# Left-over token tiles start two expert tiles later in a decoder layer's expert stage; first expert rows turned inside the last attention turn

## The chip, the cores and the metric

The kernel runs on one core of one Trainium2 chip. The metric is the device time of one execution in microseconds (us). Engines are named as in the profile: PE (TensorE, matmuls), DVE (VectorE), ACT (ScalarE), POOL (GpSimd) and SP, which only issues DMA transfers.

## What is computed

One post-norm decoder layer on x of shape 4 x 1024 x 256, in float32, with a context of 4 x 77 x 256:

```python
x = layernorm(x + self_attention(x, w_q, w_k, w_v, w_o))           # 16 heads of 16
x = layernorm(x + cross_attention(x, ctx, Wq, bq, Wk, bk, Wv, bv)) # one head of 256
# experts: 8, two for each token
gate = softmax(xf @ gate_w + gate_b); topv, topi = top_k(gate, 2); topv /= topv.sum(-1)
y = sum over e of combine[:, e] * (relu(xf @ w1[e] + b1[e]) @ w2[e] + b2[e])
x = layernorm(x + y)
```

## The kernel before

**Attention stage.** For each of 64 (batch, head) pairs there are 8 score tiles of 128 x 1024. Each tile is computed twice: `score_max` (L942) writes it to one of the two-bank PSUM tensors `pa[0]`, `pa[1]`, from where DVE takes the maxima (`maxima`, L1308), and `score_exp` (L954) writes its two halves to the banks `pb[0]`, `pb[1]`, from where ACT takes the exponentials (L1122). `sums` (L965) multiplies the exponentials with the values into `po`. Two score tiles are a "pair" (256 in all), eight pairs are a "turn" (32 in all). Maxima run `LEAD` = 8 pairs ahead, so the last turn has no `score_max` left. In every pair there is a place for one side job on PE in the bank `px` (`side`, L908): the projections of the next batch, and one step of the chain that a finished token tile `j` of 128 tokens goes through: `proj`, `turn_1`, `score` (cross scores, with a bias row added by a matmul of one row, L878), `turn_p`, `cross`, `turn_2`, `gate`. A side job waits until the reader of the one before has emptied `px` (`read_by`, L397). Token tile `j` is served `DELAY` = 9 turns after turn `j`, so 9 of the 32 token tiles are left over when attention ends: tile 23 (`MAIN_PROJ`) has its first steps to come, tile 22 (`MAIN_GATE`) its last ones.

**Expert stage.** 71 expert tiles of 128 rows follow. PE's order for expert tile t is `up(t+1)` (32 matmuls in three chunks), `turn_x(t+2)` (two transposes), `down(t)` (16 matmuls in three chunks). Between the chunks stand the steps of the left-over token tiles, `j = NT - TB + tile`, that is token tile 24 in expert tile 0. DVE copies the first-layer weights of the next expert into `w1_e` (`copy_w1`, L1650), two copies for a tile, the first of them not before `up` of the tile before has ended. The region of `w1_e` is that of the attention output of the batches 0 and 2. Which rows and which expert belong to a tile stands in a table: `early_tiles` (L1470) makes the entries of the first `EARLY` = 24 tiles from the batches 0 and 1, in turn 30; `late_tiles` (L1511) makes the other 47 after the last token tile is routed.

**Where attention ends.** The output of the last head goes out to memory and comes back turned (`store_out`, `load_out`), its row sums are inverted on DVE (`reciprocals`), written out (`spread_recs`), read back spread over the heads (`load_reps`, 512 KB), and POOL multiplies (`scale_heads`). Only then can token tile 24 be projected. On DVE the second pair of weight copies, `copy_w1(1, ..)`, stands behind `reciprocals`, and the loop over the expert tiles begins with a wait for `scaled`. Of the eight second-layer weights (1 MB each) two are loaded from SP and three from ACT at this place. ACT issues its three ahead of `copy_x(0)`, which PE needs for `up(0)`.

**Routing of the last batch.** In expert tile 9 DVE runs `counts`, `positions`, `rows`, `weights`, `pads` and all of `late_tiles`, ahead of the next `copy_w1`. `rows` writes `pos_i`, which the second scatters of the batch before still read, and waits for them:

```python
if b:
    dve.wait_ge(second_rows[b - 1], 16 * TB)
dve.tensor_copy(pos_i[:, :, :], pos_f[:, :, :]).then_inc(route, 1)
```

Of the kernel before, what the change touches and what calls it, by code (L numbers as in the profile page):

```python
# [116 lines left out]
def stream(nc, g):  # L117
# [44 lines left out]
    EARLY = 3 * TB  # L162
# [40 lines left out]
    with ExitStack() as st:  # L203
# [37 lines left out]
        fold_b = sb("fold_b", [1, B * C])  # L241
# [42 lines left out]
        pos_i = sb("pos_i", [P, 2, TB], I32)  # L284
        weight = sb("weight", [P, 2, TB])
        pad_i = sb("pad_i", [P, NE], I32)
        full_i = sb("full_i", [P, NE], I32)
        full, tiles, cum, early, step = (sb(n, [P, NE]) for n in ("full", "tiles_e", "cum", "early", "step"))
# [22 lines left out]
        pX = po[:, 0:D].rearrange("p (k t) -> p k t", k=KD)  # L311
# [85 lines left out]
        def read_by(p):  # L397
# [4 lines left out]
            if weights_step(p) is not None:  # L402
                return weights_made, weights_step(p) + 1
            if s == 0 and b:
                return rest_done, nth(b, p // TURN % TB)
# [12 lines left out]
        with nc.Block() as block:  # L418
            @block.sync
            def _(sp):  # L420
# [132 lines left out]
                for i in range(NH):  # L553
# [53 lines left out]
                for b in range(2):  # L607
                    sp.wait_ge(second_rows[b], 16 * TB)
                sp.wait_ge(table_1, len(TABLE))
                for tile in range(XS):  # L610
                    load_xg(tile)
                sp.wait_ge(v_ready, NH)
                settle(sp, g.settled_dma)
                load_w2(sp, 5)
                sp.wait_ge(b_done, 2 * TB * (NH - 2))
                settle(sp, g.settled_dma)
                load_w2(sp, 0)
                store_out(NH - 1)
                load_out(NH - 1)
                store_x2(MAIN_GATE)  # L620
                spread_recs(NH // PER - 1)
                load_reps(NH // PER - 1)
                load_x1(MAIN_PROJ + 1)
                for tile in range(FFN_TILES):
                    j = NT - TB + tile
# [7 lines left out]
                    if j + 1 < NT:  # L633
                        load_x1(j + 1)
                    if j - 1 < NT:
                        store_x2(j - 1)
                    if tile == TB + 2:
# [12 lines left out]
            def _(pool):  # L650
# [68 lines left out]
                def scatter_first(b, t):  # L719
# [3 lines left out]
                    pool.indirect_dma_start(g.xe_dram, bass.IndirectOffsetOnAxis(pos_i[:, 0, t:t + 1], 0),  # L723
                                            pay[b % 2][:, t, :], None, bounds_check=X_ROWS - 1).then_inc(first_rows[b], 16)

                def reweight(b):
                    pool.wait_ge(first_rows[b], 16 * TB)
                    pool.tensor_copy(pay[b % 2][:, :, D + 1], weight[:, 1, :]).then_inc(reweighted, 1)
# [3 lines left out]
                def scatter_second(b, t):  # L732
                    pool.indirect_dma_start(g.xe_dram, bass.IndirectOffsetOnAxis(pos_i[:, 1, t:t + 1], 0),  # L733
# [55 lines left out]
                scale_heads(NH // PER - 1)  # L789
                for tile in range(FFN_TILES):  # L790
                    j = NT - TB + tile
                    if tile:
                        scatter(tile - 1)
                    if j - 1 < NT:
                        spread_2(j - 1)
                    if j < NT:
                        spread_1(j)
                    if 2 <= tile < 6:
                        scatter_first(B - 2, 2 * (tile - 2))
                        scatter_first(B - 2, 2 * (tile - 2) + 1)  # L800
                    if 6 <= tile < 10:
                        if tile == 6:
                            reweight(B - 2)
                        scatter_second(B - 2, 2 * (tile - 6))
                        scatter_second(B - 2, 2 * (tile - 6) + 1)
                    if 10 <= tile < 14:
                        scatter_first(B - 1, 2 * (tile - 10))
                        scatter_first(B - 1, 2 * (tile - 10) + 1)
                    if 14 <= tile < 18:
                        if tile == 14:  # L810
                            reweight(B - 1)
                        scatter_second(B - 1, 2 * (tile - 14))
                        scatter_second(B - 1, 2 * (tile - 14) + 1)
# [9 lines left out]
            def _(pe):  # L823
# [48 lines left out]
                def score(j):  # L872
# [5 lines left out]
                    pe.matmul(out, g.ones[0:1, :], fold_b[:, cols], start=False, stop=True).then_inc(scored, 1)  # L878
# [28 lines left out]

                def side(p):  # L908
# [8 lines left out]
                    if weights_step(p) is not None:  # L917
                        cross_weights(weights_step(p))
                    elif s == 0:
# [34 lines left out]
                def score_exp(n):  # L954
# [57 lines left out]
                def turn_x(tile):  # L1012
                    pe.wait_ge(xg_in[tile % XS], 16 * (tile // XS + 1))
                    if tile:
                        pe.wait_ge(x_taken, tile)
                    for k in range(KD):
                        mm = pe.transpose(pX[:, k, :], xg[tile % XS][:, k * P:(k + 1) * P], g.ident[:, :])  # L1017
                    mm.then_inc(turned_x, 1)

# [37 lines left out]
                turn_x(1)  # L1057
                score(MAIN_PROJ)
                gate(MAIN_GATE)
                up(0, CHUNKS[2])  # L1060
                for tile in range(FFN_TILES):
                    j = NT - TB + tile
# [4 lines left out]
                    if j - 1 < NT:  # L1067
# [3 lines left out]
                    if j - 1 < NT:  # L1071
# [3 lines left out]
                    if j < NT:  # L1075
                        pe.wait_ge(mixed, j)
                        proj(j)
                    if tile == 1:
                        ranks(B - 2)
                    if tile == TB + 1:  # L1080
# [6 lines left out]
                    if j - 1 < NT:  # L1087
                        if j < NT:
                            pe.wait_ge(added, j + 1)
                        if tile == 1:  # L1090
# [3 lines left out]
                    if j < NT:  # L1094
# [3 lines left out]
                    if j < NT:  # L1098
                        score(j)
                    if j - 1 < NT:  # L1100
# [3 lines left out]
            def _(act):  # L1104
# [12 lines left out]
                def exponentials(n):  # L1117
                    for half in range(2):
# [3 lines left out]
                        act.activation(ex[:, n % 4, half * HALF:(half + 1) * HALF], pb[half][:, :], ACT.Exp,  # L1122
# [47 lines left out]

                def behind(p):
# [5 lines left out]
                    if n is not None:  # L1177
                        if n < KD:
                            act.wait_ge(weights_mm, n + 1)
                            act.activation(c_k[:, n, :], px[:, 0:B * C], ACT.Identity, bias=c_bk[:, n:n + 1]  # L1180
                                           ).then_inc(weights_made, 1)
                    elif s == 0 and b:
# [38 lines left out]
                def copy_x(tile):  # L1221
                    act.wait_ge(turned_x, tile + 1)
                    if tile >= 2:
                        act.wait_ge(up_done, tile - 1)
                    act.copy(xgT[tile % 2][:, :, :], pX).then_inc(x_taken, 1)

# [25 lines left out]
                for tile in range(FFN_TILES):  # L1252
                    j = NT - TB + tile
# [548 lines left out]
```

## Time and profile before

| | |
|---|---|
| median of 3 runs | 1553.7 us (1552.85 to 1553.7) |
| the profiled execution | 1560.21 us, of which 1558.4 us are the span of its instructions |
| PE busy | 1470.9 us, 94% of the span |
| DVE, ACT, POOL busy | 967.4, 821.0, 388.7 us |
| chain that ended last | PE 86%, DVE 5%, DMA 3%, issue 2%, SP's queue 2%, ACT 1% |
| attention stage | to about 941 us |
| expert stage | to about 1515 us, then the last layer norm |

The span is cut into 40 slices of 39 us in the page; a digit is the busy share of a slice in tenths. A timeline row reads: start, duration, engine, line, operation, output<-inputs, count, and in brackets how long the engine had been idle and what ended that. A row of the chain reads: start, duration, what. "PEclk" is the granted clock of PE as a share of 2.4 GHz, so 0.5 is 1.2 GHz.

### The profile page before, as it was taken

The numbers are of one execution on the slowest core, as the hardware profiler recorded it, in microseconds if no ns is written. First come the engines' busy times: TensorE is split into PE (matmuls) and PEld (weight loads), VectorE is DVE, ScalarE is ACT, GpSimd is POOL, SyncE is SP. The second block draws the span as 40 slices with busy tenths as digits, with TensorE's granted clock in tenths as the row PEclk, the third lists the DMA queues.
The fourth block names the chain that finished last, engine by engine and source line by source line (L and its number), as shares of the span: only waits on it lengthen the run. The fifth ranks groups of instructions, "written<-read, shape, count | busy, mean of one in ns | idle before, by whom it ended". The sixth has DMA issues, their size and how long they took to land.

```text
span 1558.4 us, 32241 instructions
## 1 busy us (share of the span) xinstructions
PE 1470.9 (94%) x10682; PEld 928.9 (60%) x10682; DVE 967.4 (62%) x1678; ACT 821.0 (53%) x1966; POOL 388.7 (25%) x677
## 2 busy tenths in 40 slices
PE   7899999999999999999999996998999999999990
PEld 3244443444444444444444445887999999999990
DVE  6677777778888888788888862555332333333326
ACT  3466677776676766676766772332333333333330
POOL 1211121212212214411115211354522122122123
PEclk9799999999999999999999998999999999999995
DMA  5224122324433323322343216223322222222216
GB/s 157 82 64 140 57 83 86 115 88 127 123 103 112 104 78 103 97 79 61 83 124 103 76 36 184 57 66 90 75 50 36 42 35 39 39 36 40 37 22 222
DMA packets 112195, 130.57 MB, mean 84 GB/s; under 512 B 26048, under 2 KB 89808, under 8 KB 111904
## 3 DMA queue, kind: packets, MB, share of 16 engines
q1 hardware_dynamic: 93760, 101.68, 21.9%
q0 software_dynamic: 14000, 19.48, 7.0%
q10 hardware_dynamic: 4272, 7.34, 1.3%
q8 instruction: 89, 1.46, 0.4%
q14 instruction: 74, 0.61, 0.1%
HBM read 76.51 MB, written 51.94 MB: 82 GB/s over the span
## 4 chain that ended last, share of the span: by engine, by line
PE 86%; DVE 5%; DMA 3%; issue 2%; SPq 2%; ACT 1%; POOL 0%; DVEq 0%; POOLq 0%; another core or an unknown queue 0%; ACTq 0%
PE pa L1028 16%; PE pb L961 15%; PE po L975 15%; PE pb L1039 15%; PE pa L949 13%; PE px L826 3%; PE px L862 2%; DVE neg L1313 2%; PE px L832 1%; SPq L435 1%; PE po L1017 1%; ACT w_sb L1122 1%; PE px L899 1%; PE px L877 1%; PE px L878 1%
## 5 line engine op out<-in xcount | busy, mean ns | idle before, releaser
L1313 DVE TENSOR_REDUCE neg<-pa 128x1 f32<-128x1024 f32 x512 | 614.6, 1217 | 141.8 <-PE pa L949 130.8
L1122 ACT ACTIVATE w_sb<-pb 128x512 f32<-128x512 f32 x1024 | 555.9, 595 | 207.0 <-PE pb L961 201.2
L1233 ACT ACTIVATE space<-pa,b1T_sb 128x128 f32<-128x128 f32 x568 | 154.7, 383 | 325.4 <-PE pa L1028 324.6
L961 PE MATMUL pb<-w_sb 99*128 99x512 bf16 x1024 | 314.4, 384 | 9.1 <-ACT w_sb L1122 4.9
L949 PE MATMUL pa<-w_sb 96*128 96x512 bf16 x1024 | 301.6, 385 | 8.1 <-DVE neg L1313 7.3
L1028 PE MATMUL pa<-xgT,attn_t 128*128 128x128 f32 x2272 | 274.3, 279 | 12.7 <-issue 4.9
L1028 PEld LDWEIGHTS pa<-xgT,attn_t 128*128 128x128 f32 x2272 | 271.4, 195 | 17.0 <-issue 8.5
L975 PE MATMUL po<-w_sb,space 128*32 128x256 f32 x4096 | 274.1, 385 | 0.5 <-ACT w_sb L1122 0.5
L1039 PE MATMUL pb<-w_sb,space 128*128 x1136 | 260.1, 380 | 0.0
L1039 PEld LDWEIGHTS pb<-w_sb,space 128*128 128x128 f32 x1136 | 209.5, 191 | 25.0
L1654 DVE COPY attn_t<-w_sb 128x1024 f32 x142 | 99.0, 697 | 171.9 <-PE pa L1028 156.1
L783 POOL DMA_INDIRECT x<-space,y_tag x71 | 110.4, 1554 | 376.7 <-DVE space L1671 307.8
L961 PEld LDWEIGHTS pb<-w_sb 99*128 99x128 bf16 x1024 | 82.2, 97 | 202.2 <-ACT w_sb L1122 140.8
L975 PEld LDWEIGHTS po<-w_sb,space 128*32 128x32 f32 x4096 | 106.8, 109 | 137.5 <-issue 90.2
L949 PEld LDWEIGHTS pa<-w_sb 96*128 96x128 bf16 x1024 | 96.3, 100 | 120.4 <-DVE neg L1313 27.1
L1667 DVE TENSOR_TENSOR space<-pb,b_sb 128x256 f32<-128x256 f32 x71 | 30.2, 425 | 139.2 <-PE pb L1039 132.9
L679 POOL TENSOR_TENSOR neg_parts<-neg,ones 128x8 bf16<-128x8 f32 x64 | 13.1, 205 | 262.8 <-DVE neg L1313 262.8
L714 POOL TENSOR_TENSOR dev_B<-mv_B,eps 128x1 f32<-128x1 f32 x32 | 8.6, 268 | 256.0 <-DVE mv_B L1377 256.0
L826 PE MATMUL px<-w_sb,space 128*128 128x512 f32 x96 | 46.9, 611 | 0.0
L862 PE MATMUL px<-woT_sb,attn_t 128*128 128x256 f32 x128 | 34.2, 390 | 6.0 <-DVE pay L1366 6.0
L723 POOL DMA_INDIRECT x_by_expert<-pay,pos_i x32 | 34.0, 1063 | 14.6 <-issue 10.2
L733 POOL DMA_INDIRECT x_by_expert<-pay,pos_i x32 | 33.9, 1061 | 11.2 <-issue 7.5
(194 smaller groups left out, 986.3 us busy)
## 6 DMA issues: line engine op xcount, KB each, us to landing
xg<-x_by_expert SPq DMA_DIRECT2D x71, 130.0 KB
attention_out<-space SPq DMA_DIRECT2D x64, 128.0 KB
w_sb<-w SPq DMA_DIRECT2D x16, 512.0 KB, 5.0
q_parts<-w_sb SPq DMA_DIRECT2D x48, 128.0 KB
w_sb<-q_parts SPq DMA_DIRECT2D x64, 96.0 KB, 2.5
w_sb<-k_parts SPq DMA_DIRECT2D x64, 96.0 KB, 2.5
k_parts<-w_sb SPq DMA_DIRECT2D x45, 128.0 KB
w_sb<-w SPq DMA_DIRECT2D x5, 1024.0 KB, 8.4
```

The lines of the kernel that those rows point to most:

```text
L783: pool.indirect_dma_start(g.x2_dram, bass.IndirectOffsetOnAxis(y_tag[tile % TAGS][:, 0:1], 0), y[tile % 2], None, bounds_check=Y_ROWS - 1, ...
L826: mm = pe.matmul(out[:, :], w_qk[:, which, k, m * P:(m + 1) * P], x[:, k, cols], start=k == 0, stop=k == KD - 1)
L862: mm = pe.matmul(px[:, 0:D], g.attn_t[:, b % 2, k, t * P:(t + 1) * P], g.woT_sb[:, k, :], start=k == 0, stop=k == KD - 1)
L949: mm = pe.matmul(pa[n % 2][:, half * HALF:(half + 1) * HALF], qs[i % RING][0:STACK, t * P:(t + 1) * P], ks[i % RING][0:STACK, half * HALF: ...
L961: pe.matmul(pb[half][:, :], ks[i % RING][:, t * P:(t + 1) * P], qs[i % RING][:, half * HALF:(half + 1) * HALF], start=True, stop=True).the ...
L975: mm = pe.matmul(po[32 * j:32 * j + VW, 0:QC], vs[i % 2][:, t, :], ex[:, n % 4, j * QC:(j + 1) * QC], start=t == 0, stop=t == TB - 1, tile ...
L1028: mm = pe.matmul(pH[tile % 2][:, f, :], w1_e[:, k, f * P:(f + 1) * P], xgT[tile % 2][:, k, :], start=k == 0, stop=k == KD - 1)
L1039: mm = pe.matmul(pY[tile % 2], hT[tile % 2][:, f, :], g.w2_sb[:, bass.ds(e, 1), f, :].rearrange("p e d -> p (e d)"), start=f == 0, stop=f ...
L1122: act.activation(ex[:, n % 4, half * HALF:(half + 1) * HALF], pb[half][:, :], ACT.Exp, scale=SCALE).then_inc(e_done, 1)
L1233: ins = act.activation(hT[tile % 2][:, f, :], pH[tile % 2][:, f, :], ACT.Relu, bias=g.b1_sb[:, bass.ds(e * FT + f, 1)])
L1313: dve.tensor_reduce(neg[i % 2][:, t:t + 1], pa[n % 2][:, :], AX.X, ALU.max, negate=True).then_inc(max_done, 1)
L1654: dve.tensor_copy(w1_e[:, k], g.w1_sb[:, bass.ds(e, 1), k].rearrange("p e f -> p (e f)")).then_inc(w1_copied, 1)
```

## The change

1. **Two tiles later.** `SHIFT = 2`: the steps of the left-over token tiles stand in expert tile `j + 2 - 24`. Tiles 22 and 23 are finished inside the loop (in expert tiles 1 and 2) and no longer ahead of it; routing of batch 2 moves from expert tile 1 to 3, that of batch 3 from 9 to 11, its scatters from tiles 10 to 17 to tiles 12 to 19. DVE's wait for `scaled` moves behind the weight copies of expert tile 1, with `result(0)` behind it; `scale_heads` of the last heads moves to POOL's tile 1.
2. **First rows turned early.** `turn_x(0)` and `turn_x(1)` become side jobs of the pairs 0 and 3 of the last turn, in `px`, and `copy_x(0)`, `copy_x(1)` follow the exponentials there. The first three `load_xg` stand in SP's iteration 60, `early_tiles` in turn 29. `EARLY` is 25. SP's two loads of second-layer weights stand at the end of its iteration 63.
3. **The start of the stage.** After the last `sums`, PE does `proj(23)`, waits for the maxima and does the whole of `up(0)`. DVE's first copies wait for `proj(23)` alone.
4. **Second sets of buffers.** `pos_i` and `weight` are doubled, so that `rows` and `weights` wait for the scatters of two batches before.
5. **`late_tiles` and `pads` spread.** Counts to weights of batch 3 are in expert tile 11; `pads` and stage 0 of `late_tiles` in 12, stage 1 in 13, stage 2 in 14.
6. **Bias over 128 rows.** `fold_b` is 128 rows high, zero but for its first row, and the matmul that adds it takes 128 rows.
7. **Last scores in the banks of the maxima.** From the second pair of the last turn on, `score_exp` uses the four banks of `pa` in place of the two of `pb`.

```diff
-    EARLY = 3 * TB
+    EARLY = 3 * TB + 1
+    SHIFT = 2
+    def feeds(p):
+        turn, s = divmod(p, TURN)
+        return (0, 3).index(s) if turn == TURNS - 1 and s in (0, 3) else None
+    def in_pa(n):
+        return n >= 2 * (PAIRS - LEAD) + 2
...
+        pX = [bank[:, 0:D].rearrange("p (k t) -> p k t", k=KD) for bank in (px, px, po)]
+        def score_bank(n, half):
+            return pa[n % 2][:, half * HALF:(half + 1) * HALF] if in_pa(n) else pb[half][:, :]
...
+                    if i == NH - 4:
+                        for b in range(2):
+                            sp.wait_ge(second_rows[b], 16 * TB)
+                        sp.wait_ge(table_1, len(TABLE))
+                        for tile in range(XS):
+                            load_xg(tile)
+                    if i == NH - 1:
+                        sp.wait_ge(v_ready, NH)
+                        settle(sp, g.settled_dma)
+                        load_w2(sp, 5)
+                        sp.wait_ge(b_done, 2 * TB * (NH - 2))
+                        settle(sp, g.settled_dma)
+                        load_w2(sp, 0)
...
-                    pe.matmul(out, g.ones[0:1, :], fold_b[:, cols], start=False, stop=True).then_inc(scored, 1)
+                    pe.matmul(out, g.ones[:, :], fold_b[:, cols], start=False, stop=True).then_inc(scored, 1)
...
-                        if n:
+                        if in_pa(n):
+                            pe.wait_ge(max_done, NH * TB - 1 + n % 2)
+                            pe.wait_ge(e_done, 2 * n - 3 + half)
+                        elif n:
                             pe.wait_ge(e_done, 2 * n - 1 + half)
-                        pe.matmul(pb[half][:, :], ks[i % RING][:, t * P:(t + 1) * P],
+                        pe.matmul(score_bank(n, half), ks[i % RING][:, t * P:(t + 1) * P],
...
-                pe.wait_ge(max_done, NH * TB)
-                pe.wait_ge(e_done, 2 * NH * TB)
                 pe.wait_ge(mixed, MAIN_PROJ)
                 proj(MAIN_PROJ)
-                pe.wait_ge(o_out, NH)
-                turn_x(0)
-                pe.wait_ge(added, MAIN_PROJ + 1)
-                turn_2(MAIN_GATE)
-                up(0, CHUNKS[0])
-                pe.wait_ge(c_copied, MAIN_GATE + 1)
-                turn_1(MAIN_PROJ)
-                up(0, CHUNKS[1])
-                turn_x(1)
-                score(MAIN_PROJ)
-                gate(MAIN_GATE)
-                up(0, CHUNKS[2])
+                pe.wait_ge(max_done, NH * TB)
+                for chunk in CHUNKS:
+                    up(0, chunk)
+                pe.wait_ge(e_done, 2 * NH * TB)
                 for tile in range(FFN_TILES):
-                    j = NT - TB + tile
+                    j = NT - TB + tile - SHIFT
...
                 for e in (1, 2, 3):
                     load_w2(act, e)
-                copy_x(0)
-                copy_2(MAIN_GATE)
-                copy_1(MAIN_PROJ)
-                copy_x(1)
-                soft(MAIN_PROJ)
...
-                    if b:
-                        dve.wait_ge(second_rows[b - 1], 16 * TB)
-                    dve.tensor_copy(pos_i[:, :, :], pos_f[:, :, :]).then_inc(route, 1)
+                    if b >= 2:
+                        dve.wait_ge(second_rows[b - 2], 16 * TB)
+                    dve.tensor_copy(pos_i[b % 2][:, :, :], pos_f[:, :, :]).then_inc(route, 1)
...
+                g.w1_in.wait(dve, 0, g.w1_loads)
+                e = number(dve, 0, 1)
+                dve.wait_ge(projected, MAIN_PROJ + 1)
+                for k in range(KD):
+                    copy_w1(0, k, e)
                 norm_2(MAIN_GATE)
                 add(MAIN_PROJ)
                 measure_1(MAIN_PROJ)
-                g.w1_in.wait(dve, 0, g.w1_loads)
-                for k in range(KD):
-                    copy_w1(0, k)
-                norm_1(MAIN_PROJ)
-                reciprocals(NH // PER - 1)
                 keep(0)
                 keep(1)
-                dve.wait_ge(scored, MAIN_PROJ + 1)
-                logits(MAIN_GATE)
-                cross_max(MAIN_PROJ)
-                best(MAIN_GATE)
+                norm_1(MAIN_PROJ)
+                e = number(dve, 1, 1)
+                reciprocals(NH // PER - 1)
                 for k in range(KD):
-                    copy_w1(1, k)
-                dve.wait_ge(scaled, NH // PER)
+                    copy_w1(1, k, e)
...
+                    if tile == 1:
+                        dve.wait_ge(scaled, NH // PER)
+                        result(0)
...
                         pads()
-                        late_tiles()
-                    if tile == TB:
-                        hot_experts(B - 1)
+                    if tile >= TB + SHIFT + 2:
+                        late_tiles(tile - TB - SHIFT - 2)
```

## Rows read from the trace of the kernel before

**Rows 1.** The page, part 2: PE's busy tenths in 40 slices

```profile
PE   7899999999999999999999996998999999999990
```

**Rows 2.** Chain that ended last, 320 to 917 us, shares by line

```profile
by line: PE pb L961 25.7%; PE po L975 25.2%; PE pa L949 22.8%; DVE neg L1313 4.3%; PE px L826 4.0%; PE px L862 3.0%; issue 2.7%; PE px L832 2.0%; PE px L899 1.2%; ACT w_sb L1122 1.2%; PE px L886 1.1%; PE px L877 1.1%; PE px L878 1.0%; PE px
```

**Rows 3.** Stretches: length, PE, PEld, DVE, ACT, POOL busy, PEclk, DMA share, GB/s

```profile
916.70:941.00 24.30, 21.49 (x197) 9.37 (x196) 6.07 (x20) 18.62 (x39) 2.94 (x10) 1.00 0.22 64
941.00:970.20 29.20, 16.91 (x96) 15.25 (x97) 7.28 (x23) 6.80 (x24) 4.44 (x7) 0.84 0.69 209
...
1091.60:1500.00 408.40, 408.40 (x2815) 384.96 (x2814) 127.47 (x282) 139.16 (x513) 101.27 (x71) 1.00 0.24 42
```

**Rows 4.** Chain that ended last, end of attention: start, us, what

```profile
937.01 0.39 PE pb L961
...
939.90 1.11 PE po L975 x16
...
941.43 6.67 DMA attention_out<-space
...
948.56 5.70 DMA o_sums<-attention_out
...
954.28 0.56 DVE o_sums L1324
...
964.68 2.35 POOL attn_t L700
...
967.87 2.08 PE px L862 x4
```

**Rows 5.** Timeline of PE, 941 to 1000 us

```profile
947.68 2.93 PE L1028 MATMUL pa<-xgT,attn_t 128*128 128x128 f32 x12 [4.70 <-ACT xgT L1225]
...
957.89 2.90 PE L1028 MATMUL pa<-xgT,attn_t 128*128 128x128 f32 x12 [3.10 <-DVE attn_t L1654]
...
993.53 1.13 PE L862 MATMUL px<-woT_sb,attn_t 128*128 128x256 f32 x4 [1.78 <-DVE pay L1366]
```

**Rows 6.** Timeline of SP's queue, 930 to 945 us

```profile
938.04 1.02 SPq L379 DMA_DIRECT2D w_sb<-w  x2
```

**Rows 7.** Timeline of ACT, 940 to 948 us

```profile
941.14 6.08 ACTq L379 DMA_DIRECT2D w_sb<-w  x3
```

**Rows 8.** Chain that ended last, three kinds of expert tiles

```profile
1033.78 1.44 PE pa L1028 x12
...
1044.71 1.44 PE pa L1028 x12
...
1080.22 4.91 issue
1085.13 6.42 PE pa L1028 x32
...
1095.23 3.57 PE pa L1028 x32
...
1102.47 3.57 PE pa L1028 x32
```

**Rows 9.** Timeline of DVE, 1075 to 1085 us

```profile
1075.49 0.17 DVE L1447 CAST pos_i<-pos_f 128x16 int32<-128x16 f32 x1 [2.53 <-DMA x_by_expert<-pay,pos_i]
...
1081.57 0.18 DVE L1548 TENSOR_SCALAR table<-x 128x47 int32<-128x47 f32 x1
...
1083.58 1.46 DVE L1654 COPY attn_t<-w_sb 128x1024 f32 x2 [0.42 <-issue]
```

**Rows 10.** Timeline of PE in single matmuls, around one score bias

```profile
1054.34 0.39 PE L877 MATMUL px<-fold,turned_B 128*128 128x77 f32 x2
...
1054.45 0.28 PE L877 MATMUL px<-fold,turned_B 128*128 128x77 f32 x1
...
1054.66 0.44 PE L878 MATMUL px<-fold_b,ones 1*128 1x77 f32 x2
...
1055.03 0.28 PE L899 MATMUL px<-gate_w_sb,turned_C 128*128 128x8 f32 x1
```

More of the change, by code:

```diff
@@ L283, in stream @@
         pos_f = sb("pos_f", [P, 2, TB])
-        pos_i = sb("pos_i", [P, 2, TB], I32)
-        weight = sb("weight", [P, 2, TB])
+        pos_i = [sb(f"pos_i{i}", [P, 2, TB], I32) for i in range(2)]
+        weight = [sb(f"weight{i}", [P, 2, TB]) for i in range(2)]
         pad_i = sb("pad_i", [P, NE], I32)
         full_i = sb("full_i", [P, NE], I32)
-        full, tiles, cum, early, step = (sb(n, [P, NE]) for n in ("full", "tiles_e", "cum", "early", "step"))
+        tiles, cum, early, step = (sb(n, [P, NE]) for n in ("tiles_e", "cum", "early", "step"))
+        full = cum
         b2_sb = sb("b2_sb", [P, NE, D])
@@ L403, in read_by @@
                 return weights_made, weights_step(p) + 1
+            if feeds(p) is not None:
+                return x_taken, feeds(p) + 1
             if s == 0 and b:
@@ L1219, in _ @@
                 take_output(NH - 1)
[L1221 to L1225, printed above, removed]
                 def relu(tile):
@@ L1529, in late_tiles @@
-                    dve.tensor_scalar(step[:, NE - 1:NE], early[:, NE - 1:NE], -1.0, None, ALU.mult).then_inc(table_2, 1)
-                    dve.wait_ge(table_2, tabled_2("step_last"))
-                    dve.tensor_tensor(tiles[:, :], tiles[:, :], step[:, :], ALU.subtract).then_inc(table_2, 1)
-                    dve.tensor_tensor(past, wide(slots, False, n), wide(cum[:, :], True, n), ALU.is_ge).then_inc(table_2, 1)
-                    dve.wait_ge(table_2, tabled_2("past"))
-                    dve.tensor_reduce(expert, past, AX.X, ALU.add).then_inc(table_2, 1)
@@ L1535, in late_tiles @@
-                    dve.wait_ge(table_2, tabled_2("expert"))
-                    dve.tensor_tensor(past, past, wide(tiles[:, :], True, n), ALU.mult).then_inc(table_2, 1)
-                    dve.wait_ge(table_2, tabled_2("weighted"))
-                    dve.tensor_reduce(before_e, past, AX.X, ALU.add).then_inc(table_2, 1)
-                    dve.wait_ge(table_2, tabled_2("before"))
-                    dve.tensor_tensor(before_e, slots, before_e, ALU.subtract).then_inc(table_2, 1)
-                    dve.wait_ge(table_2, tabled_2("row"))
@@ L1542, in late_tiles @@
-                    dve.tensor_scalar(before_e, before_e, early[:, 0:1], None, ALU.add).then_inc(table_2, 1)
-                    dve.wait_ge(table_2, tabled_2("row_0"))
-                    dve.tensor_scalar(before_e, before_e, float(P), None, ALU.mult).then_inc(table_2, 1)
-                    dve.wait_ge(table_2, tabled_2("rows_128"))
-                    dve.scalar_tensor_tensor(g.table[:, 0, EARLY:], expert, float(ROWS_E), before_e, ALU.mult,
-                                             ALU.add).then_inc(table_2, 1)
@@ new lines, in late_tiles @@
+                    if stage == 1:
+                        dve.tensor_tensor(past, wide(slots, False, n), wide(cum[:, :], True, n), ALU.is_ge).then_inc(table_2, 1)
+                        dve.wait_ge(table_2, tabled_2("past"))
+                        dve.tensor_reduce(expert, past, AX.X, ALU.add).then_inc(table_2, 1)
+                        dve.wait_ge(table_2, tabled_2("expert"))
+                        dve.tensor_tensor(past, past, wide(tiles[:, :], True, n), ALU.mult).then_inc(table_2, 1)
+                        dve.wait_ge(table_2, tabled_2("weighted"))
+                        dve.tensor_reduce(before_e, past, AX.X, ALU.add).then_inc(table_2, 1)
@@ new lines, in late_tiles @@
+                    if stage == 2:
+                        dve.wait_ge(table_2, tabled_2("before"))
+                        dve.tensor_tensor(before_e, slots, before_e, ALU.subtract).then_inc(table_2, 1)
+                        dve.wait_ge(table_2, tabled_2("row"))
+                        dve.tensor_scalar(before_e, before_e, early[:, 0:1], None, ALU.add).then_inc(table_2, 1)
+                        dve.wait_ge(table_2, tabled_2("row_0"))
+                        dve.tensor_scalar(before_e, before_e, float(P), None, ALU.mult).then_inc(table_2, 1)
+                        dve.wait_ge(table_2, tabled_2("rows_128"))
+                        dve.scalar_tensor_tensor(g.table[:, 0, EARLY:], expert, float(ROWS_E), before_e, ALU.mult,
+                                                 ALU.add).then_inc(table_2, 1)
+                        dve.tensor_scalar(g.table[:, 1, EARLY:], expert, float(NE - 1), None, ALU.min).then_inc(table_2, 1)
@@ L1605, in side_taken @@
                         measure_2(j)
-                    if turn == TURNS - 2 and s in (1, 4, 5, 6):
+                    if turn == TURNS - 3 and s in (1, 4, 5, 6):
                         early_tiles((1, 4, 5, 6).index(s))
```

202 lines of the change are left out of this document (105 added, 97 removed).

## Prediction

> **What bounds the kernel now.** I read the page first: PE is busy for nine tenths or more in nearly every slice, with dents in the first slices, about 940 to 1090 us, and at the end [rows 1]. So time comes either out of PE's own work or out of those dents. The chain that ended last tells which work counts in the attention stage: from 320 to 917 us over three quarters of it are the three large matmul groups of PE, and the side jobs stand on it too (L877 1.1%, L878 1.0%) [rows 2]. A saving on PE there is mostly a saving of time. The table of stretches sizes the dents [rows 3]. In the last attention turn (916.7 to 941.0) neither PE (21.5 of 24.3 us) nor ACT (18.6) is full: they wait for each other. From 941.0 to 970.2 PE is busy for 16.9 of 29.2 us, part of it at 1.2 GHz (mean granted clock 0.84). From 1091.6 to 1500 PE is full, so there only less PE work would help. In the chain of the tiles there is a second hole, 4.91 us at 1080.22, and behind it 32 matmuls that took 6.42 us [rows 8].
>
> A profiled execution takes 1560.2 us, the runs shown 1553.7: I sum against the former and take off the 6.5 us at the end. Less than 0.2% (3 us) is about what a measurement of this kernel can't tell from no change.
>
> **Part 7, the last turn.** With two banks, the second half of a tile's scores waits for the exponential of the tile before. So the chain of a pair holds this matmul (0.39 us at 937.01) between ACT's last exponential and the sums [rows 4]. With `pa` it is ready before. A matmul of 512 columns takes about 0.2 us of this 0.39 net, since the rest is the latency that the sums then have themselves. `in_pa` starts at the second pair, and the pair with `proj` and `gate` is full on PE, so six pairs gain 0.2 us: **1.3 us**. Bounds: nothing, if ACT's added copies eat it, and 7 x 0.39 = 2.7. ACT is idle for 24.3 - 18.6 = 5.7 us in these eight pairs [rows 3], so two copies of some 0.4 us fit in. The two turnings add 0.4 us to a PE that waits there for 2.8.
>
> **Parts 1 to 3, the start of the expert stage.** Call the end of the last sums E (939.90 + 1.11 = 941.0). Before, `down(0)` begins after `proj(24)` and a turning, at 967.87 + 2.08 + 0.4 = 970.4 [rows 4], so at E + 29.4. Three waits fill this. ACT issues three loads for 6.08 us [rows 7] before it copies the first rows, and `up(0)` starts at 947.68, at half clock. `up(1)` waits for weight copies until 957.89 [rows 5]. `proj(24)` waits for the last output, its reciprocals, their way out and back and POOL's 2.35 us [rows 4].
>
> After: `proj(23)` about 1.0 us (the four matmuls of 1.13 at 993.53 [rows 5]), DVE's two copies 1.46 [rows 9] with some 0.3 of latency, `up(0)` 3.57 at full clock [rows 8]: it ends at E + 6.3. Is it at full clock? PE waits 1.8 us ahead of it. The wait of 1.78 at 993.53 left the next four matmuls at 1.13 us, while after the longer standstill ahead of 967.87 four such took 2.08 [rows 4, 5]. So I count it as warm; if not, it costs 1.5.
>
> `up(1)` needs the next copies, and these stand behind `reciprocals` as before. The chain to it is the store of 6.67 us and the way back of 5.70: inversion at E + 13.3 [rows 4]. These two ran among 5 MB of weights. SP's two, issued at 938.04 [rows 6] on the queue that the store uses too, now go some 4 us earlier, since the table reads and row loads in front of them are gone. ACT's three still go out beside the store. I take a store of about 4 and a way back of 5.2, so inversion at E + 9.7. Bounds: E + 13.3 (nothing gained) and E + 6.3 (any earlier, and the copies wait for the end of `up(0)` anyway). Add 0.56, 1.46 and 0.2: `up(1)` starts at E + 11.9. PE has then idled 5 us, so its first 12 matmuls take 2.9 us instead of 1.44 [rows 5, 8], 5.1 for all; with a turning, `down(0)` starts at E + 17.2 instead of E + 29.4. This is 12.2 us earlier, but the token steps that were done in the hole now stand in the loop: one set of them, the difference between a tile with steps (1044.71 - 1033.78 = 10.93) and one without (1102.47 - 1095.23 = 7.24), 3.7 [rows 8]. Gain **8.5 us**, from 4.9 (late inversion) to 12.1.
>
> What goes on behind it: the way out and back of the reciprocals and POOL's product took 964.68 + 2.35 - 954.28 = 12.8 us [rows 4]. DVE now waits for it after the copies of tile 1, PE at `proj(24)` in tile 2. From the inversion to the first are 2.2 + 5.1 + 0.2 + 3.5 + 3.6 + 1.5 = 16 us. It is covered with 3 us to spare; each us beyond this costs one. On POOL `scatter(0)` stands behind it, which nothing needs for two tiles.
>
> **Parts 4 and 5, the hole at 1080.** DVE waits 2.53 us for the second scatters of batch 2, ends the table only at 1081.57 + 0.18, and makes the copies for the next tile at 1083.58 [rows 9], when PE has stood since 1080.22 [rows 8]. It costs 4.91 plus 6.42 - 3.57 = 2.85 at half clock: **7.8 us**. After, the wait is on batch 1, done long before. The work from 1075.66 to 1081.75, 6.1 us, goes into four tiles, the counts and positions with about 1 us of it into tile 11 (some 3.4 us in all), at most 2.4 in any other. A tile without steps has DVE busy for 31% of 7.24 us, 2.3 [rows 3], so both fit in 7.24 us. The copies may come up to 2 us after the `up` that frees their room before PE waits. Bound: 0, if the hole comes back.
>
> **Part 6, the bias.** From the start of the last fold matmul (1054.45) to the one behind the two bias matmuls (1055.03) are 0.58 us for three matmuls; the fold matmuls, with 128 rows and as many columns, follow each other by 0.11 [rows 10]. Three of those take 0.33, so a score gains 0.25. All nine scores in the expert loop are PE-bound: 2.2 us. Of those in attention the chain holds 1.0% of 597 us, 6.0 us, at 0.37 (1054.66 to 1055.03) apiece, that is 16: 4.0 us. Together **6.3 us** [rows 2, 10], between 0 (the extra time has to do with the product, not with its rows) and 32 x 0.25 = 8.
> The Trainium skill has rules for both ends. "TensorE: Matmul & The Clock Gate", section on LDWEIGHTS, says that loading weights depends on the columns and not on the rows; by it alone the term is nothing and the time 6.3 us later. "TensorEngine Tiling (Array Packing)", Key Properties, says that a change of tiling mode drains the engine; if one row counts as such a mode, this is the 0.25. The gaps of 0.21 and 0.20 on either side of the bias, against 0.11, agree with the second.
>
> **At nothing:** `early_tiles` in turn 29 (the same DVE work among the same maxima, one turn earlier); SP's waits in iteration 60 (ahead of `load_rows` of the next head; the table is made a turn, batch 1 scattered two turns before; uncovered they would stall attention); EARLY at 25; the memset at the start.
>
> **Sum.** 1.3 + 8.5 + 7.8 + 6.3 = 23.9. 1560.2 - 23.9 = 1536.3 profiled, less 6.5 gives **1530**.
>
> **Rivals.**
> (a) The forecast, 1530; with the bounds of the start 1526 to 1534. Chance 0.60.
> (b) The bias gains nothing: 1536. For it: the trace of before holds no bias of 128 rows, so the cause of the gaps is not shown. Against: the gaps [rows 10]. Chance 0.12.
> (c) The hole comes back in tiles 11 to 14, as DVE's copies slip behind the routing again: up to 1538. For it: one of the pieces still has 3.4 us, and the copies' room is free for only 3.7 us ahead of need. Chance 0.12.
> (d) `down(0)` waits for all eight weights. ACT's three start at E as before, and the old trace only says that they were in by E + 29. If they come that late, the gain of the start is lost: 1538.5. Chance 0.07.
> (e) Slower: the last scatters stand two tiles later, in tiles 16 to 19, and SP may load tile 25's rows only after them (in tile 22). Batch 2's were in at 1075.49 [rows 9], one tile after the last was issued, so two tiles are to spare. If POOL's queue makes them late, PE stands for as long. It turns the sign from 24 + 2 x 7.24 = 38 us of lateness on; with six tiles (43 us) PE stands 29 us: 1559. Chance 0.03.
> (f) More than forecast (early inversion, all scores on the path): 1523. Chance 0.06.
>
> The range of 0.8 leaves out the tips of (e), (f) and part of (c) and (d) together: 1521 to 1541. Faster by over 0.2%: all but (e) and a mishap of several, 0.95; same 0.02; slower 0.03.
>
> **What would show it.** In the profile after: the stretch of the last turn under 23.5 us; `up(0)` in one piece some 3 us after the last sums at full clock; a hole ahead of `up(1)` ended by DVE's copies; `down(0)` at E + 17; tiles with steps of 10.7 instead of 10.93; no idle PE between tile 10 and the end; bias matmuls 0.11 apart. It is wrong if a new idle time of PE ended by DVE or a load stands at tiles 11 to 25, if the inversion comes at E + 13 or later, or if bias matmuls keep their 0.58.

## The result and the profile after

The changed kernel takes 1537.8 us (median of 4 runs, 1537.5 to 1538.2) against 1553.7: ratio 0.9895, 95% interval 0.9878 to 0.9912. That is 16 us less, where 24 were forecast. The measured time lies outside the forecast's own band of 1526 to 1534 and inside the whole range of 1521 to 1541. The first line below is the busy line of the page of after, the second PE's slices; they answer to [rows 1]. The dent in the slice of 1052 to 1091 us is gone, that at the end of attention is smaller (7 tenths busy where it was 6).

```profile
PE 1458.3 (95%) x10682; PEld 921.3 (60%) x10682; DVE 968.6 (63%) x1679; ACT 820.5 (53%) x1966; POOL 388.0 (25%) x677
...
PE   7899999999999999999999997999999999999990
```

The stretches of after, cut at its own marks: last turn, hole at the start of the expert stage, `down(0)` to `down(11)`, the tiles behind. They answer to [rows 3], but the first row starts at the first `sums` of the last turn, 3.0 us later in the turn than the row of 24.30 us there. From this mark before took 20.21 + 1.11 = 21.3 us and after 19.9.

```profile
914.73:934.60 19.87, 17.92 (x178) 8.78 (x179) 3.51 (x15) 16.32 (x37) 2.00 (x8) 1.00 0.40 118
934.60:952.53 17.93, 10.20 (x71) 9.61 (x71) 4.87 (x13) 2.54 (x9) 1.31 (x4) 0.81 0.79 245
952.53:1068.69 116.16, 111.19 (x751) 100.23 (x750) 62.85 (x209) 40.47 (x148) 49.56 (x60) 0.99 0.28 64
1068.69:1490.00 421.31, 421.31 (x2907) 397.22 (x2906) 138.31 (x333) 142.04 (x528) 111.42 (x78) 1.00 0.27 45
```

The chain of after from the last sums to `down(0)`, which answers to [rows 4]:

```profile
933.46 1.11 PE po L1010 x16
934.60 0.38 ACT space L1146
935.00 3.77 DMA attention_out<-space
938.85 0.33 SPq L500
939.23 6.04 DMA o_sums<-attention_out
945.58 0.30 DVEq L397
945.88 0.23 DVE attn_t L1671
946.31 0.69 DVE attn_t L1671
947.13 5.34 PE pa L1055 x32
952.47 0.22 PE po L935 x2
952.69 3.46 PE pb L1066 x16
```

```profile
945.29 0.55 DVE L1338 RECIPROCAL o_sums<-o_sums 128x64 f32<-128x64 f32 x1 [5.43 <-DMA o_sums<-attention_out]
```

That last row, from DVE's timeline, is the inversion. With E = 934.6: the store takes 3.77 us instead of 6.67, the way back 6.04 instead of 5.70, the inversion comes at E + 10.7 and `down(0)` at E + 18.0. PE's timeline of the same place, and of expert tile 3, in which the routing of batch 2 delays `proj`, answers to [rows 5]:

```profile
937.19 3.81 PE L1055 MATMUL pa<-xgT,attn_t 128*128 128x128 f32 x32 [1.59 <-DVE attn_t L1671]
947.13 5.34 PE L1055 MATMUL pa<-xgT,attn_t 128*128 128x128 f32 x32 [6.14 <-DVE attn_t L1671]
...
993.92 1.34 PE L882 MATMUL px<-woT_sb,attn_t 128*128 128x256 f32 x4 [2.33 <-DVE pay L1380]
...
995.48 2.77 PE L1066 MATMUL pb<-w_sb,space 128*128 x6
```

`up(0)` runs in one piece at full clock. The wait of 2.33 us at 993.92 is followed by six matmuls of `down` in 2.77 us, at half clock. In the kernel before the table delayed `up(12)`, in the second expert tile behind the routing (tile 9). The same place of after is `up(14)` behind `down(12)`, and PE's timeline shows it with no gap and at full clock; it answers to the 4.91 and 6.42 us of [rows 8]:

```profile
1075.94 3.62 PE L1066 MATMUL pb<-w_sb,space 128*128 x16
1079.39 3.73 PE L1055 MATMUL pa<-xgT,attn_t 128*128 128x128 f32 x32
```

The score bias in single matmuls of after, which answers to [rows 10]: 0.34 us from the start of the last fold matmul to the start of the one behind the bias, where it was 0.58.

```profile
964.04 0.28 PE L897 MATMUL px<-fold,turned_B 128*128 128x77 f32 x1
...
964.15 0.39 PE L898 MATMUL px<-fold_b,ones 128*128 128x77 f32 x2
...
964.38 0.22 PE L919 MATMUL px<-gate_w_sb,turned_C 128*128 128x8 f32 x1
```

### The profile page after: what moved, and what is told of

The parts are those of the page before. It is cut to its first block, busy times and chain, and to the rows that moved or that the text cites. A ratio compares the mean times of both kernels' runs of the same rounds, so it can differ in the third digit from the quotient of the medians.

```text
span 1536.0 us, 32052 instructions
## 1 busy us (share of the span) xinstructions
PE 1458.3 (95%) x10682; PEld 921.3 (60%) x10682; DVE 968.6 (63%) x1679; ACT 820.5 (53%) x1966; POOL 388.0 (25%) x677
## 4 chain that ended last, share of the span: by engine, by line
PE 83%; DVE 6%; issue 3%; DMA 2%; ACT 2%; SPq 2%; DVEq 0%; POOL 0%; POOLq 0%; ACTq 0%
PE pa L1055 16%; PE pb L1066 15%; PE po L1010 14%; PE pb L996 14%; PE pa L981 13%; PE px L846 3%; DVE neg L1327 2%; PE px L882 2%; ACT w_sb L1139 2%; PE px L852 1%; SPq L451 1%; PE po L935 1%; PE px L919 1%; PE px L906 1%; DVE w_sb L1768 1%
## 5 line engine op out<-in xcount | busy, mean ns | idle before, releaser
L1139 ACT ACTIVATE w_sb<-pb 128x512 f32<-128x512 f32 x996 | 540.3, 594 | 198.8 <-PE pb L996 196.5
L996 PE MATMUL pb<-w_sb 99*128 99x512 bf16 x996 | 306.6, 383 | 5.5 <-DMA w_sb<-minus_maxima 2.7
L1055 PE MATMUL pa<-xgT,attn_t 128*128 128x128 f32 x2272 | 270.1, 276 | 7.7 <-DVE attn_t L1671 7.7
L1055 PEld LDWEIGHTS pa<-xgT,attn_t 128*128 128x128 f32 x2272 | 267.6, 193 | 11.8 <-issue 8.3
L1671 DVE COPY attn_t<-w_sb 128x1024 f32 x142 | 93.7, 697 | 132.1 <-PE pa L1055 130.6
L741 POOL DMA_INDIRECT x_by_expert<-pay,pos_i x32 | 33.5, 1046 | 15.1 <-issue 10.7
L751 POOL DMA_INDIRECT x_by_expert<-pay,pos_i x32 | 33.2, 1038 | 11.4 <-issue 7.8
```

The source lines that it names most:

```text
L996: pe.matmul(score_bank(n, half), ks[i % RING][:, t * P:(t + 1) * P], qs[i % RING][:, half * HALF:(half + 1) * HALF], start=True, stop=True ...
L1055: mm = pe.matmul(pH[tile % 2][:, f, :], w1_e[:, k, f * P:(f + 1) * P], xgT[tile % 2][:, k, :], start=k == 0, stop=k == KD - 1)
L1671: dve.tensor_copy(w1_e[:, k], g.w1_sb[:, bass.ds(e, 1), k].rearrange("p e f -> p (e f)")).then_inc(w1_copied, 1)
```

## The experiments

Four marks in each trace make the comparison sharper than the medians: the start of the first `sums`, of the last `sums`, of `down(0)` and of `down(11)`. The last `sums` are marked by their start, 1.1 us ahead of E, which is their end. What lies ahead of the first mark varies by itself: 56.5 to 60.1 us in fourteen profiled executions.

| us | e1 (before) | after | difference |
|---|---|---|---|
| up to the first sums | 57.75 | 59.88 | varies |
| to the last sums | 874.92 | 873.58 | -1.3 |
| to `down(0)` | 30.54 | 19.07 | -11.5 |
| to `down(11)` | 121.47 | 116.17 | -5.3 |
| to the end | 466.83 | 467.30 | +0.5 |
| from the first sums on | 1493.76 | 1476.12 | -17.6 |

**e1: the kernel before once more.**

> The kernel before, unchanged, profiled once more. In the profiled execution of before, six attention turns (18 to 20, 27, 28 and a part of 17) were 0.1 to 1.6 us longer than those of the kernel after, 4.8 us in all, and this execution lay 6.5 us above the median. Theory 1: these long turns belong to single executions; this profile then has turns 19 and 20 at 28.4 us, 27 and 28 at 26.4, and lies near 1554. Rival: they belong to the kernel before and something in the change took them away; then they are here again and the profile is near 1560.

1553.9 us against 1554.1 beside it, ratio 1.0001 (0.9992 to 1.0011); span 1551.5 us. Turns 19, 20, 27 and 28 last 28.38, 28.38, 26.39 and 26.39 us, the same as in after. Theory 1 holds: the 4.9 us were that one execution's. The profile that the prediction read was 6.5 us above the median for this and for 2.3 us at the start, and to take these 6.5 us off the sum was right.

**e2: the bias over 128 rows alone.**

```diff
-        fold_b = sb("fold_b", [1, B * C])
+        fold_b = sb("fold_b", [P, B * C])
...
-                    pe.matmul(out, g.ones[0:1, :], fold_b[:, cols], start=False, stop=True)
+                    pe.matmul(out, g.ones[:, :], fold_b[:, cols], start=False, stop=True)
```

> The kernel before with the bias over 128 rows alone. My prediction put 2.2 us on the nine scores of the expert stage and 4.0 us on those of the attention stage, 6.3 us in all. Theory now: in the attention stage the 0.25 us on PE are swallowed two matmuls later, where score_max waits for DVE's maxima, so turns 9 to 16 stay at 28.38 us and only the 2.2 us of the expert stage come: 1551.5. Rival (the prediction): turns of 28.1 us and 1547.5. Second rival (rows cost nothing): 1553.7.

1552.2 against 1554.1, ratio 0.9988 (0.9979 to 0.9997). In the expert stage a tile with steps takes 10.63 us instead of 10.93 and the stretch `down(0)` to `down(11)`, with eight scores, 118.73 instead of 121.47: 2.7 us. In attention the turns 10 to 16 stay at 28.37 us (28.38), and turn 26 grows from 28.11 to 28.48. So the numbers of e2's theory hold and the prediction's 4.0 us for the attention stage fall. But what swallows them is not the wait of `score_max` for the maxima. First the chain of e1 around one score of turn 24, then that of e2 around the same one:

```profile
740.17 0.40 PE px L877 x4
740.57 0.37 PE px L878 x2
740.94 0.54 PE pa L949 x2
741.48 0.43 PE pb L961 x2
741.91 1.00 PE po L975 x16
742.91 0.54 PE pb L961 x2
```

```profile
742.32 0.24 DVE cneg L1352
...
742.80 0.19 ACT pr L1158
743.00 0.99 ACT w_sb L1122 x2
743.98 0.04 issue
744.03 0.39 PE pb L961
744.42 0.43 PE pa L949 x2
```

In e1 everything stands on PE. In e2 the chain leaves PE: DVE's maxima, the cross maximum behind them (`cneg`), ACT's softmax that waits for it, and the two exponentials that wait behind this on ACT in program order. The timelines of e1 (first four rows) and e2 (last four) show why nothing is gained:

```profile
740.20 1.23 DVE L1313 TENSOR_REDUCE neg<-pa 128x1 f32<-128x1024 f32 x1
741.35 0.23 DVE L1352 TENSOR_REDUCE cneg<-px 128x1 f32<-128x77 f32 x1
741.92 1.08 ACT L1122 ACTIVATE w_sb<-pb 128x512 f32<-128x512 f32 x2
742.85 0.61 PE L961 MATMUL pb<-w_sb 99*128 99x512 bf16 x2
...
741.17 1.23 DVE L1313 TENSOR_REDUCE neg<-pa 128x1 f32<-128x1024 f32 x1
742.32 0.23 DVE L1352 TENSOR_REDUCE cneg<-px 128x1 f32<-128x77 f32 x1
742.90 2.18 ACT L1122 ACTIVATE w_sb<-pb 128x512 f32<-128x512 f32 x4
743.56 0.85 PE L961 MATMUL pb<-w_sb 99*128 99x512 bf16 x2
```

The score begins at 740.00 in e1 and at 740.98 in e2. In both, `cneg` starts 1.3 us behind that, since DVE is at maxima of 1.23 us that stand ahead of it, and not when PE is done with the score. So ACT's second exponential ends 3.0 us behind the score's beginning in both (and in every turn from 9 to 29 but 18 and 26). In e1 this is 743.00, and the second of the two L961 matmuls, which needs its bank, starts at about 743.08 (the end of the pair less 0.38 us for one), so this second path ended 0.08 us ahead of the one on PE. In e2 PE is there about 0.25 us earlier and waits 0.24 us, and the matmul starts at 744.03, as far behind the score's beginning as in e1 to within 0.03 us. The chain doesn't show what comes second. In turn 26 `cneg` starts 2.06 us behind the score's beginning in e1 and 2.43 in e2: that is the 0.37 us by which this turn grows.

**e3: the hole alone.** The second sets of `pos_i` and `weight`, and `pads` and `late_tiles` over tiles 10 to 12 of the kernel before:

```diff
-                        pads()
-                        late_tiles()
...
+                    if tile == TB + 2:
+                        pads()
+                    if tile >= TB + 2:
+                        late_tiles(tile - TB - 2)
```

> The kernel before with the second sets of pos_i and weight and with pads and late_tiles spread over tiles 10 to 12, nothing else. Theory: the hole at tile 10 of 4.91 us idle and 2.85 us at half clock goes, and nothing takes its place: 7.8 us less, 1546. Rival: part of it comes back as smaller waits in tiles 9 to 12, or the executions outside the profile have a smaller hole: 3 to 5 us less.

1547.1 against 1554.1, ratio 0.9953 (0.9939 to 0.9966). `down(0)` to `down(11)` takes 113.41 us instead of 121.47, 8.1 less, and each tile behind tile 9 takes 7.25. Tile 10 itself gives 7.65 of it (14.90 in e1); the other 0.4 lies in the tiles before, and `down(0)` came 0.5 later, so from the first sums on it is 7.6. The medians give 7.0. The theory holds.

**e4: the last scores in `pb`.**

```diff
-        return n >= 2 * (PAIRS - LEAD) + 2
+        return False and n >= 2 * (PAIRS - LEAD) + 2
```

> The kernel after with the last scores in the two banks of pb, as before. Theory: the last turn is 1.5 us longer (20.2 us between the first and last sums instead of 18.7), and all behind it shifts by as much: 1539.3. Rival: the start of the expert stage hangs on the output's way to memory and back, which doesn't care for 1.5 us of PE: then it still shifts, since the output is finished by the same sums; only if the way back is bound by the weight loads do less than 0.5 us remain.

Between the first and last sums of the last turn lie 20.21 us instead of 18.73, and from the first sums to the end 1478.07 instead of 1476.12. The theory holds in the trace. The median, 1537.2 (0.9893, 0.9878 to 0.9908), can't show it: the start varies by more.

**e5 and e6: which half of the hole.** e5 puts `pads` and all of the table into tile 11 and keeps the two sets; e6 has one set and keeps the table spread.

```diff
-                    if tile == TB + SHIFT + 2:
-                        pads()
-                    if tile >= TB + SHIFT + 2:
-                        late_tiles(tile - TB - SHIFT - 2)
+                    if tile == TB + SHIFT + 1:
+                        pads()
+                        for stage in range(3):
+                            late_tiles(stage)
```

> The kernel after with pads and all of late_tiles in expert tile 11 behind the routing of the last batch, in place of tiles 12 to 14; pos_i and weight stay doubled. Theory: the table is the larger cause of the hole. DVE then has about 3.4 + 6.1 us in one tile and some 5.8 us of room, so PE stands for 2 to 4 us ahead of up(12) and loses up to 2.9 more at half clock: 3 to 6 us more than the kernel after. Rival: without the wait of 2.53 us there is room enough and nothing changes.

```diff
-        pos_i = [sb(f"pos_i{i}", [P, 2, TB], I32) for i in range(2)]
+        pos_i = [sb(f"pos_i{i}", [P, 2, TB], I32) for i in range(1)] * 2
...
-                    if b >= 2:
-                        dve.wait_ge(second_rows[b - 2], 16 * TB)
+                    if b:
+                        dve.wait_ge(second_rows[b - 1], 16 * TB)
```

> The kernel after with one pos_i and one weight, so that DVE waits again for the second scatters of batch 2 in tile 11, with the table still spread. Theory: a wait of some 2.5 us alone fits into DVE's room, PE does not stand: same as after (0 to 0.5 us more). Rival: the wait alone makes part of the hole: 2 us or more.

PE in e5, at `up(14)`:

```profile
1080.57 5.44 PE L1055 MATMUL pa<-xgT,attn_t 128*128 128x128 f32 x32 [2.07 <-issue]
```

2.07 us idle and 5.44 - 3.73 = 1.7 at half clock: the trace from one `down` to the next has 11.18 us instead of 7.25, 3.9 more, as the theory has it, and the median is 1540.2 (0.9914, 0.9897 to 0.9930), 2.4 above after. DVE in e6:

```profile
1073.15 0.17 DVE L1461 CAST pos_i<-pos_f 128x16 int32<-128x16 f32 x1 [2.54 <-DMA x_by_expert<-pay,pos_i]
```

The same wait as in [rows 9], 2.54 us, and PE has no gap behind it: every tile from 11 on takes 7.24 to 7.25 us. The median is 1535.4 (0.9883, 0.9867 to 0.9900). So the table at once makes a hole of 3.9 us alone, the wait makes none alone, and only with the table does it lengthen it to 7.7 us. The second sets of buffers, in the kernel after, are worth nothing that shows.

**e7: weight copies ahead of the reciprocals.**

```diff
                 e = number(dve, 1, 1)
-                reciprocals(NH // PER - 1)
                 for k in range(KD):
                     copy_w1(1, k, e)
+                reciprocals(NH // PER - 1)
```

> The kernel after with the second pair of weight copies (copy_w1(1)) ahead of reciprocals on DVE, nothing else. Theory: the 6.14 us of PE's wait ahead of up(1) come from the order on DVE alone: up(1) starts at E + 8.2 instead of E + 12.6 (E is the end of the last sums) and at full clock, down(0) at E + 12.1 instead of E + 18. But the reciprocals' way and POOL's product still end at E + 24, and DVE waits for them in tile 1 ahead of cross_max(23), so part comes back as a wait of PE ahead of turn_p(23) in tile 2: 3 to 4 us less than after in all. Rival: down(0) waits for the second-layer weights, at E + 14 or later, and less than 2 us remain.

The timeline of PE in e7, with E = 934.4:

```profile
942.42 3.81 PE L1055 MATMUL pa<-xgT,attn_t 128*128 128x128 f32 x32 [1.59 <-DVE attn_t L1671]
946.07 0.38 PE L935 MATMUL po<-ident,xg 128*128 128x128 f32 x2
948.84 1.64 PE L1066 MATMUL pb<-w_sb,space 128*128 x3 [2.38 <-DMA w_sb<-w]
```

`up(1)` starts at E + 8.0 as the theory has it. But then PE waits for the last second-layer weights until E + 14.4, and `down(0)` takes 5.36 us, most of it at half clock, instead of 3.62. From the last sums to the end it is 600.7 us against 602.5 of after: the rival was right. 1535.7 us, 0.9887 (0.9870 to 0.9903).

**e8: e7, a later wait for `scaled`, and routing over two tiles.**

```diff
-                    if tile == 1:
-                        dve.wait_ge(scaled, NH // PER)
-                        result(0)
                     if MAIN_GATE <= j - 1 < NT:
...
+                    if tile == 1:
+                        dve.wait_ge(scaled, NH // PER)
+                        result(0)
...
+                    if tile == SHIFT + 2:
                         rows(B - 2)
                         weights(B - 2)
```

> The run e7 with two more moves on DVE: the wait for scaled and result(0) stand behind logits, cross_max and best in tile 1, and rows and weights of batch 2 stand in tile 4 instead of tile 3. Theory: the rest of the 6 us arrives too, and tile 3 loses its wait of 2.3 us ahead of proj with the half clock behind it (13.9 us down to 12 or less): 7 to 8.5 us less than after. Rival: rows and weights only make tile 4 as long as tile 3 was, and the way of the reciprocals decides at proj(24) in tile 2: 4 us less than after, like e7.

1540.1 us (0.9916, 0.9899 to 0.9932): 4.4 us more than e7 and 2.3 more than after, and neither theory had it. DVE in e8:

```profile
968.95 0.17 DVE L1677 COPY y_tag<-xg 128x2 int32<-128x2 int32 x1 [3.76 <-DMA x<-space,y_tag]
```

With `result(0)` later its scatter is later (issued at 964.96, E + 31.9, against 961.46, E + 27.1, in e7), and `keep(4)`, which uses the same `y_tag` again, waits 3.76 us for it, ahead of `mix(23)`; PE stands for 3.95 us ahead of `proj(24)`. The split routing gave nothing worth having: tiles 3, 4, 5 took 11.7, 12.0, 11.9 us instead of 13.9, 11.5, 10.6.

**e9: the first of the three waits of before.**

```diff
+                copy_x(0)
                 for e in (1, 2, 3):
                     load_w2(act, e)
-                copy_x(0)
```

> The kernel before with copy_x(0) ahead of ACT's three weight loads, nothing else. It takes away the first of the three waits at the end of attention: up(0) then starts some 5 us earlier (E + 1.5 to E + 2.5, by DVE's weight copies). Theory: this alone is worth nothing, since up(1) still waits for the copies behind reciprocals and proj(24) for the reciprocals' way out and back, both of which hang on the last output: within 0.5 us of before, with the three loads and the store shifted by less than 1. Rival: each wait of PE in this stretch has its own worth, and 3 to 5 us come.

`up(0)` starts at 941.00, E + 5.1 instead of E + 6.7, held by DVE's weight copies, and not by E + 2.5 as expected. `down(0)` is 30.4 us behind the last sums, as before (30.5). 1553.7 us, 0.9999 (0.9989 to 1.0008): nothing, as the theory says.

**e10 and e11: after and e7 side by side.**

> The kernel after, unchanged, to stand beside e11 on one chip. 1537.8 as before; from the last sums to the end 602.5 us in its profile, or 1 to 1.5 less where PE stays at full clock behind the wait of 2.3 us in expert tile 3 (as it did in e5 and e6).

> The run e7 once more: copy_w1(1) ahead of reciprocals. From e7: down(0) at E + 15.5, ended by the last second-layer weights, and 1.9 us less than after from the last sums to the end. Expected 1.5 to 2.5 us less than e10.

e10: 1536.7 us (0.9891, 0.9875 to 0.9908), 602.9 us from the last sums on. e11: 1534.5 us (0.9883, 0.9866 to 0.9899), 599.7. The difference is 2.2 us in the medians and 3.2 in the traces: e11 is the fastest version here, about 1.2% under before. The same place of e10 that cost after half clock:

```profile
993.99 1.13 PE L882 MATMUL px<-woT_sb,attn_t 128*128 128x256 f32 x4 [2.34 <-DVE pay L1380]
```

The wait is the same, 2.34 us, and the matmuls behind it stay at full speed; in turn `up(1)` of e10 took 6.69 us instead of 5.34. So 1.3 us of the clock's cost stand in one place in one execution and in the other in the next.

**e12: ACT's weight loads behind `relu(0)`.**

```diff
-                for e in (1, 2, 3):
-                    load_w2(act, e)
                 act.wait_ge(table_1, len(TABLE))
                 act.wait_ge(const_in, 16 * CONSTANTS)
                 relu(0)
+                for e in (1, 2, 3):
+                    load_w2(act, e)
```

> The kernel after with ACT's three weight loads behind relu(0), 8 us later. Theory: the last output's store and way back then don't share the DMA engines with 3 MB of weights, so the inversion comes at E + 6 to E + 7.5 instead of E + 10.7 and up(1) starts by E + 9.5; but the weights land about 10 us after their issue and down(0) waits for them until E + 19 to E + 21: within 2 us of after. Rival: the way back is long for its own sake (64 KB in small pieces) and the inversion stays at E + 10 or later; then down(0) is 3 us or more later than in after.

DVE and PE in e12, with E = 934.1:

```profile
939.65 0.55 DVE L1338 RECIPROCAL o_sums<-o_sums 128x64 f32<-128x64 f32 x1 [0.24 <-issue]
```

```profile
958.80 5.71 PE L1066 MATMUL pb<-w_sb,space 128*128 x16 [12.64 <-DMA w_sb<-w]
```

Half of the theory holds: without ACT's weights beside it the output is back and DVE inverts at E + 5.6, 5 us earlier than in after, and DVE, no longer the one that waits, has the copies of tile 1 done at E + 8. The other half falls: the weights land at E + 24.6, `down(0)` starts at E + 24.7, 14.3 us after the last issue in the chain, and 1545.5 us result (0.9952, 0.9935 to 0.9968).

## Why the prediction was right in kind and too large in size

**Right:** faster, and for the reasons given. The last turn, forecast at 1.3 us, gave 1.5 (20.22 to 18.73) and e4 takes it back. The hole, forecast at 7.8, gave 8.1 in e3. PE stayed at full clock behind the wait of 1.6 us ahead of `up(0)`. It did not in every run: in e6 the same wait was 1.97 us, and `up(0)` took 5.44 us instead of 3.81. `early_tiles` cost the same in its new turn: turn 29 is 1.45 us longer, turn 30 1.48 shorter.

**The step that failed: the bias in the attention stage.** The prediction took a saving on PE to be "mostly a saving of time" there, read 16 scores off the shares of the chain and took 0.25 us for each, 4.0 us. Measured: none, and 0.4 us more in turn 26, since a path through DVE and ACT ended only 0.08 us ahead of PE's (e2). The 2.2 us of the expert stage came as 2.7. The gaps beside a bias of one row are gone in the rows of after, and e2's 10.93 to 10.63 us a tile shows that the row count is not free. The Trainium skill ("TensorEngine Tiling (Array Packing)", Key Properties) says that a change of tiling mode drains the engine. The gaps agree with that if one row counts as such a mode, but no run shows the mechanism: none has a bias of, say, 32 or 64 rows.

**A term that was mis-sized: the start of the expert stage,** 8.5 us forecast. From the last sums to `down(11)` the kernel gained 11.5 + 5.3 = 16.8 us; less 8.1 (e3) and 2.7 (e2) this leaves 6.0, and e10 gives 5.7. Two causes show in the traces. The way back took 6.04 us and not 5.2, so the inversion came at E + 10.7 instead of E + 9.7 and `down(0)` at E + 18.0 instead of E + 17.2. And the routing of batch 2, moved from tile 1 to 3, waits 2.33 us where it waited 1.78 [rows 5]; it can fall to half clock there, and then takes 13.9 + 11.5 us for two tiles, where 13.2 + 11.4 less 2 x 0.3 were to be had. In e10 PE stayed at full clock there and the two took 13.5 + 10.6, but then `up(1)` took 1.35 us longer. Tile 2 adds 0.5: 11.52 us, where the same steps took 11.03 in tile 0 of e2. Why, and where the 0.5 us behind `down(11)` come from, is open.

**Rivals.** (b), nothing from the bias, was right for the attention stage only. (c), the hole coming back, did not happen; in e5, with all of the table in one tile, 3.9 us of it came back. (d), weights as the bound, did not decide in after, where ACT's third load landed at 948.82, E + 14.2, ahead of `down(0)` at E + 18.0. But its cause is real: they bind as soon as the copies are earlier (e7). (e) did not happen: no tile from 11 on is longer than 7.25 us. So 1537.8 lies in the whole range by the room that was left for rivals; of their mechanisms only a part of (b) happened.

Sum of the terms: 1.5 + 6.0 + 8.1 + 2.7 - 0.4 - 0.5 = 17.4 us, against 17.6 between the marks and 16 in the medians. This is no check of the 6.0, which is itself what was left of 16.8. The difference to the medians lies within what the first 60 us vary. The memset of 128 rows adds nothing to them that shows: 58.5 us in the mean of the four profiled executions without it, 58.9 in that of the ten with it.

## What to carry to other kernels

A chain that runs through an engine for its whole length says what the last path is, not how far the second one lies behind. Before a saving is multiplied by its share of the chain, look for the other engines' handoffs in the same period: here one ended only 0.08 us ahead of it, and nothing of 0.25 us came through. Of several waits in one hole only the one that ends last has a worth: here the first one taken away alone gave nothing (e9), and of 4.5 us that `up(1)` came earlier in e7, another wait, for weights, left 2 to 3.

## What the runs showed of the hardware

The last of three loads of 1 MB each from ACT's queue landed 13.1 us behind its issue in e7 and 14.3 in e12. In e7 the last output was under way beside them. In e12 it was not, but 512 KB of spread reciprocals and three loads of expert rows were, so no run here shows these loads alone. The output, for its part, needed 10.3 us from the issue of its store to the inversion beside ACT's loads (935.00 to 945.29 in after) and 5.1 in e12 (934.54 to 939.65). I had taken both for victims of the same contention; the runs show it for the small transfers, and leave it open for the large ones. And the same wait of PE of 2.3 us at the same place was followed by full clock in one execution (e10) and by half clock in another (after).
